# Cross-attention and an NF4 feed-forward on one core: the weight sums of the down pass formed another way

## What is computed

```python
def dequant_nf4(q, absmax, shape):           # q: int32 codes 0..15, one scale for 64 values
    w = NF4_CODE[q.reshape(-1)]
    return (w.reshape(-1, 64) * absmax[:, None]).reshape(shape)

# x, ctx: (8, 256, 1024); gate_q, up_q: (3584, 1024); down_q: (1024, 3584)
Q = layernorm(x) @ Wq.T + bq;  K = ctx @ Wk.T + bk
x = x + softmax(Q @ K.T / 32) @ ctx
xn = layernorm(x)
h = silu(xn @ Wg.T) * (xn @ Wu.T)
out = x + h @ Wd.T
```

## The kernel before

| group | steps | weight before | held in the tiles of |
|---|---|---|---|
| 3 | 42 to 55 | Q3 - Q0 | quadrant 0 |
| 4 | 56 to 69 | Q2 - (Q3 - Q0) | quadrant 0 |
| 5 | 70 to 83 | Q2 - Q3 | quadrant 3 |
| 6 | 84 to 97 | Q1 - (Q2 - Q3 + Q0) | quadrant 1 |

## Time and profile before

### The profile page before, as it was taken

How to read it: one execution, slowest core, us unless ns; L and a number is a source line. 1 busy time by engine, 2 the same in 40 slices (tenths; PEclk the granted TensorE clock), 3 DMA queues, 4 the chain that set the end, 5 groups by cost and what they waited for, 6 DMA issues and landing times.

```text
span 2030.2 us, 29928 instructions
## 1 busy us (share of the span) xinstructions
PE 1947.2 (96%) x9872; PEld 985.3 (49%) x9872; DVE 1658.9 (82%) x2790; ACT 1499.9 (74%) x2782; POOL 410.7 (20%) x600
## 2 busy tenths in 40 slices
PE   8989999989999999999999999999998988799999
PEld 3468878744444444444444444444443433344444
DVE  6748888877898898898898888888887778896964
ACT  3768878757988988988998998897999998700000
POOL 0012644630111121121111111111231221101010
PEclk9989999999999999999999999999999999999999
DMA  9012689673645555455464655555698897762552
GB/s 340 26 42 79 183 234 218 181 271 93 145 125 119 135 137 127 122 141 125 121 158 110 133 137 128 128 129 136 156 221 212 229 238 215 160 187 99 187 187 83
DMA packets 393482, 314.63 MB, mean 155 GB/s; under 512 B 327280, under 2 KB 327280, under 8 KB 391408
## 3 DMA queue, kind: packets, MB, share of 16 engines
q1 hardware_dynamic: 347216, 159.07, 34.6%
q0 software_dynamic: 44032, 153.65, 23.9%
q10 hardware_dynamic: 2080, 0.01, 0.1%
HBM read 154.31 MB, written 82.31 MB: 117 GB/s over the span
## 4 chain that ended last, share of the span: by engine, by line
PE 37%; ACT 25%; DVE 20%; issue 10%; DMA 2%; POOL 0%; DVEq 0%; ACTq 0%; SPq 0%
PE ps L1990 18%; PE ps L2032 14%; ACT sq L274 8%; ACT sq L270 6%; DVE w L283 4%; DVE tail L2145 2%; ACT halves L321 2%; ACT tail L2063 2%; PE ps L1399 2%; DVE halves L339 2%; ACT tail L2078 1%; PE ps L1360 1%; DMA T<-halves 1%; ACT w L274 1%; DVE tail L2111 1%
## 5 line engine op out<-in xcount | busy, mean ns | idle before, releaser
L1990 PE MATMUL ps<-T,wS 128*128 128x512 f16 x4704 | 1020.0, 379 | 10.9 <-ACT ps L2047 6.5
L1990 PEld LDWEIGHTS ps<-T,wS 128*128 128x128 f16 x4704 | 458.5, 98 | 569.0 <-issue 15.7
L274 ACT ACTIVATE sq<-sq 128x512 f32<-128x512 f32 x898 | 514.0, 632 | 0.0
L283 DVE SCALAR_TENSOR_TENSOR w<-sq,w 128x512 f32<-128x512 f32 x598 | 423.4, 708 | 96.3 <-ACT sq L274 86.0
L270 ACT ACTIVATE sq<-q 128x512 f32<-128x512 int32 x598 | 366.3, 636 | 56.1 <-DVE w L283 52.8
L2032 PE MATMUL ps<-T,tail 128*128 128x512 f16 x1584 | 356.6, 387 | 33.4 <-DVE T L2173 19.8
L2032 PEld LDWEIGHTS ps<-T,tail 128*128 128x128 f16 x1584 | 156.6, 100 | 230.7 <-DVE T L2173 22.2
L321 ACT CAST halves<-w 128x512 f16<-128x512 f32 x234 | 145.3, 621 | 88.1 <-DVE w L283 77.3
L1399 PE MATMUL ps<-T 128*128 128x256 f16 x1536 | 175.8, 274 | 3.1 <-DVE T L1624 2.9
L339 DVE SCALAR_TENSOR_TENSOR halves<-w,halves 128x512 f16<-128x512 f32 x252 | 172.1, 689 | 8.0 <-ACT halves L321 6.8
L2032 PE MATMUL ps<-T,wS 128*128 128x512 f16 x768 | 170.2, 382 | 7.7 <-DVE T L2173 5.4
(11 more groups left out here) (214 smaller groups left out, 1945.8 us busy)
## 6 DMA issues: line engine op xcount, KB each, us to landing
keep_h<-tail POOLq DMA_DIRECT2D x196, 256.0 KB, 2.8
tail<-keep_h POOLq DMA_DIRECT2D x66, 512.0 KB, 4.8
wS<-keep_h POOLq DMA_DIRECT2D x32, 512.0 KB, 4.6
q<-in_L_ffn_down_q POOLq DMA_DIRECT2D x56, 256.0 KB, 4.1
q<-in_L_ffn_up_q POOLq DMA_DIRECT2D x52, 256.0 KB, 2.9
q<-in_L_ffn_gate_q POOLq DMA_DIRECT2D x48, 256.0 KB, 3.2
keep_x<-T SPq DMA_DIRECT2D x38, 256.0 KB, 2.9
T<-in_x SPq DMA_DIRECT2D x9, 1024.0 KB, 5.1
```

What stands on the lines that cost most here:

```text
L274: nc.scalar.activation(place, place, ACT.Square, bias=b, scale=a).then_inc(un.s_act, 1)
L283: nc.vector.scalar_tensor_tensor(out=un.w[:, buf, :], in0=square_place(un, u, i - 1), scalar=FACTORS[i - 1][1], in1=un.w[:, buf, :], op0=A ...
L1990: last = nc.tensor.matmul(ps[:, bank, :], un.wS[:, z % SLOTS, a, kt, :], t.Tp[side][product][:, :, b, kt, :], start=fresh and n == 0, stop ...
```

## The change

It touches the down pass alone.

- **Group 3 takes its weight from fp32.** The last factor of a unit of quadrant 0 writes its fp32 tile to `t.saved[pair]`, which is the memory of the tile that quadrant 3's unit of the same pair gets later. A new step `difference` on VectorE subtracts that tile from quadrant 3's unit in fp32, before the split into high and low part. So what is split and transposed for quadrant 3 is Q3 - Q0.
- **42 sums instead of 56**, chained: Q2 - (Q3 - Q0) into quadrant 3's tiles for group 4, then Q2 - Q3 into quadrant 0's for group 5, then Q1 less the first into quadrant 1's for group 6. They are due one per step from step 52.
- **Places.** Quadrants 2 and 3 change places, so that quadrant 3's tiles come free earlier. `tile_place` and `tile_free` say so; `not_before` holds the last factor of quadrant 0's units until the tile is free.
- **High parts.** Every second one of the down pass is on VectorE (28), not every third (18).
- **Pace.** `quota` gives 8 VectorE and 10 ScalarE instructions per down step throughout, where it gave 6 and 10 for 42 steps and 9 and 16 afterwards.

```diff
-GROUP_QUAD = (0, 1, 2, 0, 0, 3, 1)
-GROUP_SUM = (None, None, None, 0, 1, 2, 3)
+GROUP_QUAD = (0, 1, 2, 3, 3, 0, 1)
+GROUP_SUM = (None, None, None, None, 0, 1, 2)
...
 def high_on_dve(z):
-    return z >= GATE_UP_PIECES and (z - GATE_UP_PIECES) % 3 == 2
+    return z >= GATE_UP_PIECES and (z - GATE_UP_PIECES) % 2 == 1
...
+def tile_place(quad, pair):
+    n = {0: pair, 3: pair, 1: CH_PAIRS + pair, 2: CH_PAIRS + pair}[quad]
+    return int(quad > 1), n // PAIRS, n % PAIRS
+
+def tile_free(quad, pair):
+    side, product, _ = tile_place(quad, pair)
+    return slot_of(STAGES - 1, product, side) + 1
...
 def factor(nc, dve, un, t, u, i):
...
-        nc.vector.scalar_tensor_tensor(out=un.w[:, buf, :], in0=square_place(un, u, i - 1), scalar=FACTORS[i - 1][1],
+        out = un.w[:, buf, :]
+        if i == NF and GATE_UP_UNITS <= u < GATE_UP_UNITS + CH_PAIRS:
+            dve.wait_ge(t.s_mm, tile_free(3, u - GATE_UP_UNITS))
+            out = t.saved[u - GATE_UP_UNITS]
+        nc.vector.scalar_tensor_tensor(out=out, in0=square_place(un, u, i - 1), scalar=FACTORS[i - 1][1],
...
+def difference(nc, dve, un, t, v):
+    dve.wait_ge(un.s_fac, STEPS * (GATE_UP_UNITS + v + 1))
+    w = un.w[:, v % 4, :]
+    nc.vector.tensor_tensor(w, w, t.saved[v - 3 * CH_PAIRS], ALU.subtract).then_inc(un.s_dif, 1)
...
 def decode_dve(nc, dve, un, t):
...
+        if v >= 3 * CH_PAIRS:
+            yield difference(nc, dve, un, t, v)
...
 class Plan:
...
+                self.not_before[n] = HIDDEN_PHASE + tile_free(*quad_of(z - GATE_UP_PIECES))
+        for v in range(CH_PAIRS):
+            self.not_before[fac[GATE_UP_UNITS + v, STEPS - 1]] = HIDDEN_PHASE + tile_free(3, v) + 1
...
-        return (6, 10) if phase - DOWN_PHASE < 3 * CH_PAIRS else (9, 16)
+        return 8, 10
...
-SUM_AT = PLAN.sum_steps()
+SUM_AT = [4 * CH_PAIRS - 4 + n for n in range(3 * CH_PAIRS)]
...
-        left, right, place = ((3, 0, 0), (2, 0, 0), (2, 3, 3), (1, 0, 1))[which]
+        left, right, place = ((2, 3, 3), (3, 0, 0), (1, 3, 1))[which]
...
         def sum_of(n):
...
-                turned(dve, un, GATE_UP_PIECES + pair)
+                turned(dve, un, GATE_UP_PIECES + 2 * CH_PAIRS + pair)
                 turned(dve, un, GATE_UP_PIECES + 3 * CH_PAIRS + pair)
...
-                dve.wait_ge(s_wsumlo, n - CH_PAIRS + 1 if which < 3 else n - 2 * CH_PAIRS + 1)
-                if which == 1:
-                    turned(dve, un, GATE_UP_PIECES + 2 * CH_PAIRS + pair)
+                dve.wait_ge(s_wsumlo, pair + 1)
```

More of the change, by code:

```diff
@@ L370, in decode_dve @@
     for late in (4, 3, 2, 1):
-        yield piece_lo(nc, dve, un, GATE_UP_PIECES - late)
+        yield piece_lo(nc, dve, un, t, GATE_UP_PIECES - late)
     for v in range(DOWN_UNITS):
@@ L537, in quota @@
             return (2 if k // SPLIT_STEPS % 2 or k % 2 else 3), 6
-        return (6, 10) if phase - DOWN_PHASE < 3 * CH_PAIRS else (9, 16)
-    def sum_steps(self):
-        steps = []
-        for pair in range(CH_PAIRS):
-            piece = self.lo[GATE_UP_PIECES + 3 * CH_PAIRS + pair]
-            due = sum(done < piece for done in self.dve) - DOWN_PHASE + 1
-            steps.append(due)
-        return steps + [4 * CH_PAIRS - 2 + n for n in range(3 * CH_PAIRS)]
+        return 8, 10
 PLAN = Plan()
-SUM_AT = PLAN.sum_steps()
+SUM_AT = [4 * CH_PAIRS - 4 + n for n in range(3 * CH_PAIRS)]
 def sums_at(m):
@@ L614, in xattn_ffn_kernel @@
         t.Tp = [[big(place, 8).rearrange("p (b a k m) -> p b a k m", b=PAIRS, a=2, k=4) for place in places] for places in T_PLACES]
-        t.wd = [big(T_PLACES[half][c // PAIRS] + 2 * (c % PAIRS), 2).rearrange("p (a k m) -> p a k m", a=2, k=4)
-                for half in range(HALVES) for c in range(CH)]
+        tiles = [[(T_PLACES[side][product] + 2 * n) for side, product, n in (tile_place(q, pair) for pair in range(CH_PAIRS))] for q in range(4)]
+        t.wd = [[big(place, 2).rearrange("p (a k m) -> p a k m", a=2, k=4) for place in places] for places in tiles]
+        t.saved = [big(place, 2).bitcast(F32) for place in tiles[3]]
         t.A = big(0, 32).rearrange("p (a k d) -> p a k d", a=2, k=KT)
@@ L2166, in sum_of @@
             nc.vector.tensor_tensor(tmp, tmp, right[:, 1], ALU.subtract).then_inc(s_wsum, 1)
-            used = (pair, 3 * CH_PAIRS + pair, None, CH_PAIRS + pair)[which]
-            if used is not None:
-                dve.wait_ge(*down_freed(used))
+            used = (3 * CH_PAIRS + pair, pair, CH_PAIRS + pair)[which]
+            dve.wait_ge(*down_freed(used))
             dve.wait_ge(s_wsum, n + 1)
```

78 lines of the change are left out of this document (45 added, 33 removed).

## The result

| | before | after |
|---|---|---|
| median (lowest to highest), us | 2031.16 (2028.58 to 2041.62) | 2007.39 (2005.07 to 2016.3) |
| ratio to before, 95% interval | | 0.9881 (0.9842 to 0.9921) |
| profiled execution, its span | 2032.03, 2030.2 | 2016.3, 2014.5 |
| down pass, from step 0 to TensorE's end | 563.1 | 547.3 |
| VectorE busy | 1658.9 | 1626.2 |

The kernel became 1.2% faster, 23.8 us by the medians. The profiled execution of the changed kernel is 9 us above its own median, so it shows more waiting than is usual; a second profiled execution of the same kernel is therefore read beside it (the last experiment). So places in the down pass are compared from step 0, and the length of the pass is given beside each median.

The account below looks back on a forecast made before the run. TensorE, busy nearly throughout, bounds the kernel; only holes can be won. Step 55 at 1782 plus 43 steps x 5.18 = 222.7 ends TensorE at 2004.9, 21.7 us less; 2009 given between 2011 and a lighter 2003, range 1998 to 2023.

Parts of the forecast that it names:

- The sums leave group 3: Steps 42 to 51: VectorE stops being the bound in group 3; all of the 35.7 us lost there could go.
- The wait at step 14: End of group 0: VectorE's copies and additions come 3.3 us later (5.4 - 2.1).
- Step 33 "stays": Group 2: the wait stays, its unit's transpose standing on SP's queue behind eight loads of y; 5.5 us before.
- The late start: Start of down pass: decode 6.7 us late at unit 9's end (bounds 5.4 and 8.8), about 2.2 at unit 45.
- Rival C: Late start costs all its 8.8 us, at group ends and in group 3's feed: 2016, within 1%; chance 0.10.
- The transposes: Group 3: unit 46's transpose, behind the loads of y, lands after 13 us; 8 us wait, 2 of lower clock.
- ScalarE, last square at 1760 to 1764: End of the decode: unit 55 squared at 1760 to 1764, so step 55 can start at 1774 at the earliest.
- Rival A: Group 3: ScalarE's feed alone decides, the transpose behind the loads landing in under 6 us: 2003; chance 0.22.
- Rival B: Group 3: DMA engines are the bound, late transposes cost a further 8 to 12 us: 2017 to 2023; chance 0.13.
- Even pace: Group ends: VectorE's copies and additions stand behind decode instructions, 3.3 us later at step 14, 2.9 at step 28.
- High parts: Down pass: 28 instead of 18 on VectorE, ScalarE's unit 5.46 us, worth 5.2 us over the pass.
- Rival D: Group 3: TensorE waits nearly every step, clock stays at 1.2 GHz, 5.18 us more per step: above 2053; chance 0.06.

Follow-up runs that it names:

- the last experiment: The changed kernel run once more, unaltered, as control and second look: 2012.13 us, ratio 0.9911 to the kernel before.
- saved elsewhere: Changed kernel, but quadrant 0's units 0 and 1 are saved in the idle buffers of sums 1 and 2, so the decode starts earlier: 2000.21 us, 0.984.
- saved elsewhere, old pace: The kernel saved elsewhere, with the pace of before (6 and 10 for 42 steps, then 9 and 16): 2013.85 us, 0.991.

## Why the prediction was right, and where only by balance

The direction and the size came true: 2009 said, with a range of 1998 to 2023, 2007.39 and 2012.13 measured. Counted from step 0, the pass was forecast at 541.5 us (the forecast's end of 2004.9 is 0.2 more than 1782 + 222.7), and the two executions took 547.3 and 538.2. That is in part luck. Step 42 was forecast 240.2 us after step 0 and came 3.4 and 5.7 later; steps 42 to 47 were forecast at 42.1 us (1740.5 + 5.18 - 1703.6) and took 2.5 more in the one execution and 9.0 less in the other. Its steps, in their order:

- **The sums leave group 3.** Right. No wait ends on a sum, VectorE falls from 79.33 to 73.12 us of 88. The 35.7 us of steps 42 to 51 became 13.5, and 2.0 in the second execution.
- **The wait at step 14, "3.3 later".** Too small: step 14 began 79.7 us after step 0 before, 85.1 and 85.5 in the two executions of the change, 5.4 and 5.8 later. The copies stand behind 94 factors of the down units in the kernel before and 93 in the change, with 18 low parts in both. With the early start it is 98 factors and 82.4 us (saved elsewhere), and 92 factors and 75.9 us (the same, old pace). At 1.1 us per factor (5.5 per unit) both say about 77 us for 93 factors, so an estimate of the late start's cost here is 8.2 us, and what else the change does gives 2.8 back. I had 6.7 for the one, and 1.3 and 2.1, 3.4 in all, for the other. Step 28 (2.9 forecast, 5.1 and 5.6 measured from step 0) carries it on.
- **Step 33 "stays".** Right: 7.5 and 8.2 us, before 5.5, behind a transpose that took 16.7 and 17.2 to land. That it would vanish with one or two units more of lead I had not seen.
- **The late start, 6.7 us.** The bounds were 5.4 and 8.8, and it lies near the upper one: ScalarE began unit 9 28.4 us after step 0, where it was 20.3 before and 19.9 with the units saved elsewhere. It shrinks less than was forecast: units 18, 31 and 45 began 7.1, 5.1 and 5.2 us later than before, where 5.4, 3.1 and 2.2 were said. What the late start costs at the end is 7 to 12 us by the medians, because a shorter lead also uncovers transposes, at step 33 and at steps 44 to 46. Rival C's mechanism is true in size. Its time of 2016 is not the kernel's: the medians are 2007.39 and 2012.13, and two of its eight executions took as long (2016.3 and 2016.91).
- **The transposes.** Right in part. The neighbour rows gave 13 us; unit 46 took 15.7 and 9.3, unit 33 16.7 and 17.2. Forecast were one late transpose and 10 us. In the first execution there were three waits, 8.5 us together and 13.5 lost with the slower steps behind them, but two of the three, at steps 44 and 45, ended on transposes ahead of the loads; in the second one wait of 1.8 us and 2.0 lost. That transposes are late where the loads of y are is shown by moving the loads. That the order in the queue makes them late is supported (units 34 and 35) and not isolated. The upper bound of 17.5 us was itself a sign of that: it is unit 51's transpose, issued at 1759.0, long after the last load of y (1724.1). Beside it went out, among others, five loads of h from GpSimd's queue (1758.3 to 1762.2), the last three of which took 12.7 to 14.3 us. By the Trainium skill's page DMA: Bandwidth & Descriptors, section on queues, rings and completion order, descriptors of one ring are taken in order. The traces agree with it as far as they show: in groups 2 and 3 of both executions of the change the transpose right behind the loads landed after the last of them, by 0.8 to 7.1 us.
- **ScalarE, last square at 1760 to 1764.** From step 0 that is 296.6 to 300.6 us; it was 305.4 and 301.6. Unit 45 began 3.0 us later than forecast in both. The 2.96 us behind the additions were in the forecast, the waits for codes in group 3 (0 to 4 us) took 4.6 in the first execution.
- **Rival A.** In the second execution the feed was nearly the bound: the last transpose landed at 1780.9, half a microsecond ahead of step 55, which began at 1745.17 + 7 x 5.18 = 1781.4, 315.3 after step 0. Rival A said 310.6, the forecast 318.6, the first execution 324.4. A's condition, a landing in under 6 us behind the loads, was met in neither (15.7 and 9.3). Its mechanism, the feed alone, is seen where the loads were moved.
- **Rival B.** Not settled. The DMA share of the stretch was 0.91 (0.68 before, 0.98 in group 2), and in the first execution units 45 and 46 landed after 13.9 and 15.7 us while a load on the other queue took 13.4, which is B's mechanism; its time, 2016.3, lies just under B's 2017 to 2023. In the second execution group 3 had one short wait, and no run varied the traffic alone.
- **Even pace, taken for a delay of 3.3 us at step 14 and 2.9 at step 28.** This is the step that failed. I saw no gain in the pace; the runs show a gain of 27 to 32 us by the medians (22 to 28 by the ratios) in the changed kernel and of 14 with the early start. The sum came out right because it took for granted that VectorE, once freed, would let the decode run ahead. With the old pace it cannot: it stands 8.8 to 9.7 us at the additions, which the change has put two units earlier in its program. What I should have asked is where each engine stands in its program when the group ends.
- **High parts, 5.2 us.** Not seen: none with a third (0.9881), none with all (0.9843 against 0.984); the intervals leave room for 5 us.
- **After group 3.** Right, no hole from step 48 to the end, though two sums were made before unit 55's decode was done.
- **Rival D.** The clock of the stretch rose from 0.86 to 0.94; behind waits of 2.8 to 8.9 us the next 24 or 48 matmuls lost 1.7 to 2.9 us, and those after them ran at full pace. So D did not come.

Neither the sum nor the pace is worth anything alone (0.999 without the sum, 1.0019 without the pace); together they are worth 0.988.

## What to carry to other kernels

Where every engine's program is written out, a block that needs two engines (here the additions, which need TensorE's group done and stand among the decode) has a best place, and a plan's quota moves it: too early, and the engine stands in front of it and holds up all that is behind (8.8 to 10 us each); too late, and the consumer waits for every unit put ahead of it (5.5 us each, 24 us at step 14 with pace 9 of 12). A change that starts the feeder later moves that place too, here by a unit, though no line of the quota is touched. Price a pace in both directions, in units of the feeder, even where it looks like bookkeeping. And count the lead at the place where a late transfer will be needed: one or two units of lead hid a transfer that moving loads between queues or steps only made late elsewhere, so a buffer that lets the feed start earlier (0.984) was worth more than either move (0.990, 0.991).

## What the runs showed that I had not expected

Over all these traces, a transpose issued right behind the eight loads of y on its own queue takes 7.0 to 20.1 us to land (20.1 is unit 32, saved elsewhere, old pace), and at one place (unit 46) 9.3 in one execution and 15.7 in another, its issue alone 5.0 and 10.4. Transposes with no such loads ahead of them are late at times too: 17.5 us (unit 51 before), 13.9 (unit 45), 12.4 (unit 50 with the loads on GpSimd's queue). A kernel whose lead is thin at such a place spreads: the two executions of the changed kernel differ by 9.1 us in the length of the pass.
